# Attention of a 16-image block: scores and maximum products written in four pieces of 32 output rows

## The reference

```python
def _L0_conv_ref(x, qkv_w, proj_w, proj_b):
    ...
    xt = x.reshape(B, C, N).transpose(0, 2, 1)
    qkv = jnp.einsum('bnc,oc->bno', xt, qkv_w)
    qkv = qkv.reshape(B, N, 3, NUM_HEAD, DIM_HEAD).transpose(2, 0, 3, 1, 4)
    q, k, v = (qkv[0], qkv[1], qkv[2])
    attn = jnp.einsum('bhnd,bhmd->bhnm', q, k) * SCALE
    attn = jax.nn.softmax(attn, axis=-1)
    out = jnp.einsum('bhnm,bhmd->bhnd', attn, v)
    out = out.transpose(0, 2, 1, 3).reshape(B, N, C)
    out = jnp.einsum('bnc,oc->bno', out, proj_w) + proj_b
    return out.transpose(0, 2, 1).reshape(B, C, H, W)
x = x + _L0_conv_ref(_gn(x), L0_conv_qkv_w, L0_conv_proj_w, L0_conv_proj_b)
```

## Time and profile before

| | us |
|---|---|
| median of 3 runs (lowest, highest) | 1629.27 (1627.18, 1630.3) |
| the profiled execution's own time | 1626.17 |
| its span, first to last instruction | 1624.4 |
| PE busy | 1502.3 |
| POOL busy | 1319.5 |
| ACT busy | 1197.5 |
| DVE busy | 1164.1 |

### The profile page before, as it was taken

One profiled execution on the slowest core, in us unless ns is written; L12 is line 12 of the kernel. 1 busy time (PEld: TensorE's weight loads), 2 busy tenths in 40 slices (PEclk: granted clock), 3 DMA queues, 4 the chain that ended last, 5 costly groups with the idle time before them and its releaser, 6 DMA issues.

```text
span 1624.4 us, 24488 instructions
## 1 busy us (share of the span) xinstructions
PE 1502.3 (92%) x8800; PEld 514.2 (32%) x8800; DVE 1164.1 (72%) x2022; ACT 1197.5 (74%) x2001; POOL 1319.5 (81%) x645
## 2 busy tenths in 40 slices
PE   3379999999999999999999999999999999999872
PEld 1123233333333333333333333333333333333210
DVE  3387868778787877877786877877787887877500
ACT  2138787877869787887978787887968787777750
POOL 4028898988989898998989898998989898888880
PEclk9989999999999999999999999999999999999985
DMA  2304051352616043251515144251615223141112
GB/s 73 59 27 86 22 94 39 78 88 54 106 41 116 24 103 57 63 102 54 105 41 105 28 94 72 57 108 35 117 37 100 45 76 64 54 86 37 30 46 59
DMA packets 86105, 108.86 MB, mean 67 GB/s; under 512 B 38240, under 2 KB 50912, under 8 KB 85984
## 3 DMA queue, kind: packets, MB, share of 16 engines
q1 hardware_dynamic: 85984, 107.30, 32.2%
HBM read 42.98 MB, written 13.15 MB: 35 GB/s over the span
## 4 chain that ended last, share of the span: by engine, by line
PE 62%; DMA 9%; ACT 8%; POOL 5%; SPq 5%; issue 2%; DVE 2%; POOLq 0%; DVEq 0%; ACTq 0%
PE heads_ps L561 16%; PE max_ps L470 14%; PE scores_ps L546 14%; DMA sums_spread<-sums_sb 7%; PE extra_ps L520 6%; ACT probs L675 4%; PE extra_ps L529 3%; SPq L351 3%; POOL prob_pairs L728 2%; POOL prob_pairs L734 2%; PE extra_ps L533 2%; PE extra_ps L531 2%; PE extra_ps L530 2%; PE extra_ps L534 2%; SPq L428 1%
## 5 line engine op out<-in xcount | busy, mean ns | idle before, releaser
L675 ACT ACTIVATE probs<-scores_ps,exp_scale 128x512 f32<-128x512 f32 x1536 | 974.8, 698 | 292.5 <-PE scores_ps L546 287.2
L829 DVE TENSOR_REDUCE half_max<-max_ps 128x1 f32<-128x512 f32 x1536 | 981.1, 682 | 290.2 <-PE max_ps L470 279.9
L728 POOL TENSOR_TENSOR prob_pairs<-probs 128x1024 f32<-128x1024 f32 x384 | 896.3, 2360 | 173.9 <-ACT probs L675 173.2
L470 PE MATMUL max_ps<-k_stack,q_stack 96*128 96x512 f16 x1536 | 588.1, 384 | 23.9 <-DVE half_max L829 14.8
L546 PE MATMUL scores_ps<-q_stack,k_stack 98*128 98x512 f16 x1536 | 581.7, 380 | 14.0 <-DMA q_stack<-shift_rows 8.1
L561 PE MATMUL heads_ps<-probs,v_sb 128*32 128x512 f32 x3072 | 410.7, 607 | 1.5 <-ACT probs L675 0.8
L470 PEld LDWEIGHTS max_ps<-k_stack,q_stack 96*128 96x128 f16 x1536 | 150.3, 98 | 297.5 <-issue 104.2
L734 POOL TENSOR_TENSOR prob_pairs<-prob_pairs 128x1024 f32<-128x1024 f32 x96 | 224.2, 2357 | 0.0
L546 PEld LDWEIGHTS scores_ps<-q_stack,k_stack 98*128 98x128 f16 x1536 | 150.2, 98 | 182.2 <-ACT probs L675 34.1
L520 PE MATMUL extra_ps<-prob_pairs,ones 128*32 128x512 f32 x1152 | 134.0, 598 | 5.8 <-POOL prob_pairs L728 5.8
L561 PEld LDWEIGHTS heads_ps<-probs,v_sb 128*32 128x32 f32 x3072 | 61.0, 108 | 152.4 <-issue 130.5
(11 more groups left out here) (82 smaller groups left out, 956.8 us busy)
## 6 DMA issues: line engine op xcount, KB each, us to landing
q_stack<-qk_hi SPq DMA_DIRECT2D x96, 128.0 KB, 4.2
k_stack<-qk_hi SPq DMA_DIRECT2D x96, 128.0 KB, 5.8
inv_sb<-inv_rows SPq DMA_DIRECT2D x48, 256.0 KB
x_res<-x SPq DMA_DIRECT2D x16, 768.0 KB, 5.4
out<-x_res SPq DMA_DIRECT2D x16, 768.0 KB, 4.8
x_sb<-x SPq DMA_DIRECT2D x16, 512.0 KB, 6.7
x_sb<-x SPq DMA_DIRECT2D x32, 256.0 KB, 8.0
q_stack<-qk_lo SPq DMA_DIRECT2D x48, 128.0 KB, 4.5
```

The costliest lines, as they stand in the source:

```text
L470: pe.matmul(max_ps[:, bank, :], q_stack[0:STACK, par, h, P * tile:P * (tile + 1)], k_stack[0:STACK, par, h, HALF * half:HALF * (half + 1)] ...
L675: nc.scalar.activation(probs[:, a, s % RING, HALF * half:HALF * (half + 1)], scores_ps[:, u_bank(s, u), :], ACT.Exp, scale=exp_scale[:, 0: ...
L728: nc.gpsimd.tensor_tensor(prob_pairs[:, a, q, :], probs[:, a, (s - 1) % RING, :], probs[:, a, s % RING, :], ALU.add).then_inc(pairs_added, 1)
L829: nc.vector.tensor_reduce(half_max[:, a, tile, half:half + 1], max_ps[:, bank, :], AX_X, ALU.max).then_inc(max_read[bank], 1)
```

## The change

A score product and a maximum product are each written as four products of 32 output rows, with the same moving operand, into the same bank. The weights are cut in pieces of 32 columns, and each piece writes its own 32 partitions. The wait stays ahead of the first piece and the semaphore is raised by the last. The 128 output rows of all extras but the sums stay as they are.

```diff
@@ row_max
                     pe.wait_ge(max_read[bank], g)
-                pe.matmul(max_ps[:, bank, :], q_stack[0:STACK, par, h, P * tile:P * (tile + 1)],
-                          k_stack[0:STACK, par, h, HALF * half:HALF * (half + 1)],
-                          start=True, stop=True).then_inc(max_filled[bank], 1)
+                for at in range(0, P, D):
+                    last = pe.matmul(max_ps[at:at + D, bank, :],
+                                     q_stack[0:STACK, par, h, P * tile + at:P * tile + at + D],
+                                     k_stack[0:STACK, par, h, HALF * half:HALF * (half + 1)],
+                                     start=True, stop=True)
+                last.then_inc(max_filled[bank], 1)
@@ score
                     pe.wait_ge(probs_ready, g - SCORE_BANKS + 1)
-                pe.matmul(scores_ps[:, u_bank(s, u), :],
-                          k_stack[0:SHIFTED, st.parity, h, P * tile:P * (tile + 1)],
-                          q_stack[0:SHIFTED, st.parity, h, HALF * half:HALF * (half + 1)],
-                          start=True, stop=True).then_inc(scores_ready, 1)
+                for at in range(0, P, D):
+                    last = pe.matmul(scores_ps[at:at + D, u_bank(s, u), :],
+                                     k_stack[0:SHIFTED, st.parity, h, P * tile + at:P * tile + at + D],
+                                     q_stack[0:SHIFTED, st.parity, h, HALF * half:HALF * (half + 1)],
+                                     start=True, stop=True)
+                last.then_inc(scores_ready, 1)
```

## The result

| us | before | after |
|---|---|---|
| median of 4 runs each (lowest, highest) | 1629.0 (1627.18, 1630.3) | 1644.88 (1641.63, 1648.29) |
| the profiled execution | 1626.17 | 1641.63 |
| its span | 1624.4 | 1639.8 |

The kernel became slower by 15.9 us: 1.0099 of the time before, with a 95% interval of 1.0073 to 1.0124. The forecast was 1647 us and slower. The profiled pair differs by 15.5 us, where the sum said 18.2.

The account below looks back on a forecast made before the run. TensorE (PE) was taken to bound the middle of the run; 32.3 + 15.0 - 11.3 - 11.5 - 3.3 - 3.0 = +18.2 us gave 1644 from the profiled execution, 1647 us against the median, range 1617 to 1686.

Parts of the forecast that it names:

- Rounds: Each score or maximum product as four side-by-side pieces: 0 extra per round of 0.215 to 0.22 us, at most 9 us in all.
- Switches: PE's changes between 128- and 32-wide products: V and QK slots +0.22 us each (+32.3), projection slots +0.25 (+15.0).
- rival 2: Unseen f16 switches around product halves are cheap, so the kernel gets faster: 1583 us if they cost nothing; 12%.
- rival 3: Switch cost belongs to f32 products however placed, so nothing moves: 1629 us; 8% with rival 2's break-even zone.
- Saved stays: Stretches in another output width that disappear, -0.24 us each: sums slots -11.3 us, slots 23, 0 and 1 -11.5.
- What absorbs: Existing waits taking up growth: slot 8's second half, before slot 9, -3.3 us; slot 14's wait on the sums' DMA -3.0.
- Sum: Whole kernel: switches, saved stays and absorbed waits together make it +18.2 us slower.
- Rival 1: PE's instruction issue becomes the bound, 8 instructions per 0.22 us round: 1750 us, or 1970 if not evened out; 8%.

Follow-up runs that it names:

- the repeats: The kernel before and the changed kernel, both unaltered, run and profiled a second time: 1631.91 and 1645.83 us.

## Why the prediction was right, and where its steps were off

**Rounds: nothing extra.** Right: a round takes 0.22 in every view.

**Switches.** Right in kind and sign: the f16 switches, which no row had shown, cost 0.09 in and 0.11 out. So rival 2 (cheap f16 switches) and rival 3 (f32 alone) are out, by the timeline and by the scores alone in pieces. The term was too large by an eighth: I took 0.12 to leave, and with the first product's 0.01 a product slot should have grown by 0.22 or 0.25; free of waits it grew by 0.19 or 0.22. Leaving costs 0.11. The rule of the Trainium skill (page "TensorEngine Tiling (Array Packing)", section "Tiling Modes") that a change of mode drains the engine agrees with this trace for f16 and for all three widths tried, as far as a gap goes: 0.31 to 0.34 between starts instead of 0.22. The page gives no price, and the draining itself is seen in no profile.

**Saved stays.** Right for sums (-0.24) and slot 1; slots 23 and 0 gave 0.08 and 0.12 of 0.24. "It hardly fits, but fits" was too much. The timeline of PE and its weight loads in slot 23 of the changed kernel:

```profile
856.71 0.39 PE L550 MATMUL scores_ps<-q_stack,k_stack 98*32 98x512 f16 x4
857.08 0.10 PEld L471 LDWEIGHTS max_ps<-k_stack,q_stack 96*32 96x32 f16 x4 [0.47 <-DVE half_max L834]
857.08 0.40 PE L471 MATMUL max_ps<-k_stack,q_stack 96*32 96x512 f16 x4
857.31 0.39 PE L550 MATMUL scores_ps<-q_stack,k_stack 98*32 98x512 f16 x4
```

The maximum product starts 0.37 us behind the score instead of 0.22; it waits for its bank, which DVE reads. That maxima then wait more for DVE shows in the waits, too (from 28.7 us to 41.6 in all). In slot 0 it is ACT: the first value products of a new pair of heads wait until ACT has copied the heads before them (L654), and in each of twelve images they start 0.14 behind the end of that copy and 0.44 behind the score instead of 0.22. The forecast counted exponentials and maxima there, but not this copy nor DVE's other work.

**What absorbs.** Slots 8 and 9 together came out at -0.01 for a forecast 0. Slot 14 absorbed more than I took: -0.30 (-0.20 between the repeats) for +0.02. The wait's cause, the DMA behind a row of stacks, is shown by moving the stack. Its shrinking was mis-sized: slots 10 to 13 grew by 0.13 in all, and the wait fell by 0.49, from 0.66 to 0.17. The DMA was issued as long behind slot 10's value products as before (6.0 us), but DVE's read of it came 10.2 us behind the issue instead of 10.8 (means of the twelve middle images); why the move was faster stays open. Slot 18's wait of 0.15 went, too, and slot 7's shrank, which I had not counted.

**Sum.** The total came out near the forecast in part by luck. A middle image grew by 0.62 and 0.69 us in the two pairs of profiles; the steps made 1.34 (six QK at 0.22, four projections at 0.25, slots 7, 11 at 0.22, slot 14 at 0.02, less six at 0.24). Twelve such images gave 7.4 and 8.2 us where that makes 16.1; the first two and the last two gave 3.7 and 6.2 where the sum had about 2. The body as a whole grew by 11.2 and 14.5 us for the 18 said. To this comes the lead-in, which I left at nothing and whose pieces cost 5.5 to 6 us by the medians. Its seven product slots stand among maxima, so they have stays of their own there, 7 x 2 x 0.21 = 2.9 us as an estimate; that removing the pieces there makes the kernel faster is shown, that these stays are the cost is argued, and they explain half of it. What was too high in the middle and what was left out at both ends are of like size, and they met.

**Rival 1, issue.** Out: V rounds at 10 ns an instruction, where I had 41 as the fastest pace shown and feared 27. The pace that I took from the V products was set by their columns: in pieces, with four times the instructions, a V round still takes 0.083. The 62 ns of sequencer work per matmul that the Trainium skill (page "TensorE: Matmul & The Clock Gate", section on the 56 ns gap) gives without hardware decoding are not seen: four matmuls start every 0.083 us, and slot 8 of the kernel all in pieces holds 80 matmuls in 3.43 us, 43 ns each.

## What to carry to other kernels

Count the changes of output width, not the products: between products of 128, 64 and 32 output rows each change costs PE about 0.1 us here, f16 or f32, and a change that makes one neighbour alike can make two others unlike. So try all products of an inner loop alike before some of them: in this kernel scores and maxima alone lost 1%, the same with everything else in pieces gained 1%, and with one DMA moved out of the way 1.7%. What a saved gap is worth is set by the engine that is late next: here the 87 us of gaps that all products in pieces save gave 34. And a wait that is removed can uncover the next one, as in slot 15 when the stack was moved.

## What was not expected of the hardware

- Four products of 192 columns side by side, with their four weight loads, start every 0.083 us; 40 instructions in a row keep 10 ns each, and 160 in a slot 21 ns each.
- Weight loads of 32 columns for the round to come go on under the running round of the same rows and add nothing to its 0.22, and they are as long as those of 128 columns were (mean 96 against 98 ns).
- The first product behind a change is 0.25 ahead of the second with 96-column weights, 0.22 to 0.23 with 128 columns, and at most 0.23 with 32 in f16. The load of 96 columns is the longest, 119 ns against 95 to 97 for the 128 of a QK product, and two of them one behind the other take more than a pass; that this is the reason is argued.
- How long PE stays at its lower level in the first 120 us differs between executions of one kernel (13 and 29 us of the last 40), and the start of the body moves with it by 4 us, a quarter of what was to be measured. The granted clock in the view of stretches is 1.00 there even while the products start at half pace.
